# Attention scores of a one-layer language-model tower: one 32-row matmul per head instead of a zero-padded 128-row matmul per four heads

## What is computed

```python
q = _bitlinear(x, w_q).reshape(B, T, N_HEADS, D_HEAD)      # 32 sequences, T = 128, 16 heads of 32
k = _bitlinear(x, w_k).reshape(B, T, N_HEADS, D_HEAD)
v = _bitlinear(x, w_v).reshape(B, T, N_HEADS, D_HEAD)
attn = jnp.einsum('bqhd,bkhd->bhqk', q, k) * D_HEAD ** (-0.5)
attn = jax.nn.softmax(attn, axis=-1)
out = jnp.einsum('bhqk,bkhd->bqhd', attn, v).reshape(B, T, C)
return _bitlinear(out, w_o)
```

## Time and profile before

| | |
|---|---|
| median of three runs | 1735.05 us |
| span of the profiled execution (first to last instruction) | 1725.5 us |
| the rest of the time, median less span | 9.6 us |
| TensorE busy | 1609.2 us, 93% of the span |
| VectorE busy | 1195.8 us, 69% |
| ScalarE busy | 957.5 us, 55% |
| GpSimd busy | 632.1 us, 37% |
| in the attention stage, 290 to 760 us: TensorE / VectorE / ScalarE / GpSimd | 456.0 / 419.1 / 350.4 / 220.0 of 470 us |
| the copies into `KTx`, 320 to 740 us (29 sequences): GpSimd / ScalarE | 112.1 / 18.1 us |
| the score matmuls in the same stretch | 104.3 us |

### The profile page before, as it was taken

The page is one execution under the profiler, slowest core; times in us unless marked ns, Lnnn a source line. Parts: engine busy times, 40 slices in busy tenths (PEclk is TensorE's granted clock), DMA queues, the critical chain, the costliest instruction groups (busy, mean ns, idle before and its releaser), DMA issues.

```text
span 1725.5 us, 33624 instructions
## 1 busy us (share of the span) xinstructions
PE 1609.2 (93%) x10884; PEld 1354.1 (78%) x10884; DVE 1195.8 (69%) x2292; ACT 957.5 (55%) x1936; POOL 632.1 (37%) x614
## 2 busy tenths in 40 slices
PE   1798886999999999969999999999999999999997
PEld 0444444777777777749999999999999999999996
DVE  2687886999999999866343566666666666655665
ACT  4976774777777777753222355555555555522221
POOL 4655533544444444421750122222222222023343
PEclk9999999999999999989999999999999999999999
DMA  9999981000000000013111366677766777534365
GB/s 311 315 340 341 337 276 53 26 38 37 36 36 36 36 36 31 37 68 115 37 38 49 121 218 232 234 243 251 251 232 234 238 247 247 207 127 139 109 206 196
DMA packets 89868, 274.42 MB, mean 159 GB/s; under 512 B 12640, under 2 KB 13152, under 8 KB 89696
## 3 DMA queue, kind: packets, MB, share of 16 engines
q1 hardware_dynamic: 70688, 223.71, 37.5%
q0 software_dynamic: 17024, 45.97, 8.8%
q10 hardware_dynamic: 2112, 4.19, 0.8%
HBM read 228.14 MB, written 45.69 MB: 159 GB/s over the span
## 4 chain that ended last, share of the span: by engine, by line
PE 54%; DMA 1%; DVE 0%; POOL 0%; ACT 0%; issue 0%; POOLq 0%; DVEq 0%
PE up_ps L1372 12%; PE up_ps L1370 12%; PE up_ps L1371 12%; PE down_ps L1370 6%; PE down_ps L1371 6%; PE down_ps L1372 6%; PE xT_ps L1414 2%; DMA comb<-slot_rows,slot_i 0%; DVE H L1320 0%; DMA xr<-x_turned 0%; DVE xT_lo L1237 0%; POOL comb L1172 0%; ACT xT_hi L1187 0%; DVE H L1312 0%; PE route_ps L1366 0%
## 5 line engine op out<-in xcount | busy, mean ns | idle before, releaser
L1370 PE MATMUL up_ps<-xT_hi,w_hi 128*128 128x256 f32 (+1 forms) x1704 | 483.9, 284 | 8.4 <-DVE xT_lo L1237 8.4
L1372 PE MATMUL up_ps<-xT_hi,w_lo 128*128 128x256 f32 (+1 forms) x1704 | 481.1, 282 | 0.0
L1371 PE MATMUL up_ps<-xT_lo,w_hi 128*128 128x256 f32 (+1 forms) x1704 | 479.1, 281 | 0.0
L1370 PEld LDWEIGHTS up_ps<-xT_hi,w_hi 128*128 128x128 f32 (+1 forms) x1704 | 308.1, 181 | 10.0 <-DVE xT_lo L1237 8.5
L1371 PEld LDWEIGHTS up_ps<-xT_lo,w_hi 128*128 128x128 f32 (+1 forms) x1704 | 308.1, 181 | 1.2
L1372 PEld LDWEIGHTS up_ps<-xT_hi,w_lo 128*128 128x128 f32 (+1 forms) x1704 | 308.1, 181 | 0.0
L1242 DVE TENSOR_TENSOR w_lo<-w_stage,w_hi 128x1408 fp32r<-128x1408 f32 (+1 forms) x123 | 201.4, 1664 | 124.4 <-ACT w_hi L1192 124.2
L1164 POOL DMA_INDIRECT xr<-x_rows,slot_tokens x78 | 120.5, 1544 | 441.6 <-PE xT_ps L1414 362.2
L1219 ACT ACTIVATE h_hi<-h 128x256 fp32r<-128x256 f32 (+1 forms) x213 | 89.0, 418 | 239.3 <-DVE h L1335 239.3
L279 DVE TENSOR_TENSOR W<-W,norm_ps 128x1000 f32<-128x1000 f32 x128 | 147.1, 1190 | 53.5 <-PE norm_ps L354 53.3
L1215 ACT ACTIVATE act_g<-up_ps 128x256 f32<-128x256 f32 (+1 forms) x213 | 79.6, 374 | 182.8 <-PE up_ps L1372 181.4
(11 more groups left out here) (192 smaller groups left out, 2978.0 us busy)
## 6 DMA issues: line engine op xcount, KB each, us to landing
W<-table_t SPq DMA_DIRECT2D x32, 2000.0 KB, 17.2
w_stage<-packed SPq DMA_DIRECT2D x80, 704.0 KB, 6.5
w_stage<-packed SPq DMA_DIRECT2D x40, 768.0 KB, 5.2
slot_rows<-y_rows SPq DMA_DIRECT2D x39, 512.0 KB, 6.7
xr<-x_turned SPq DMA_DIRECT2D x32, 512.0 KB, 3.7
x_rows<-x SPq DMA_DIRECT2D x32, 256.0 KB, 2.0
x_turned<-x2T SPq DMA_DIRECT2D x32, 256.0 KB, 2.0
out<-H SPq DMA_DIRECT2D x32, 256.0 KB, 3.7
```

The lines of the kernel that those rows point to most:

```text
L1370: pe.matmul(out, a_hi, b_hi, start=first, stop=False)
L1371: pe.matmul(out, a_hi, b_lo, start=False, stop=False)
L1372: return pe.matmul(out, a_lo, b_hi, start=False, stop=last)
```

## The change

Q and K columns are laid out anew (on the host, by a transposition of the two weight matrices' columns): head 4j + m now lies on partitions 32j to 32j + 31 of block m, so that the four heads of one block lie on four row strips of TensorE and belong to four different groups, hence four PSUM banks. Each head's scores are a matmul of its own with 32 rows, 128 weight columns and 128 moving columns, 16 in place of 4, in the order block m outside, strip j inside. `scores_done` is raised only in the last block, once per group. `KTx`, its zeroing, its copies on GpSimd and ScalarE and their semaphores are gone; `K_T` becomes a pair of buffers.

```diff
-        K_T = sb("K_T", [P, KT, T])
-        KTx = pair("KTx", [P, KT, GROUPS, T])
+        K_T = pair("K_T", [P, KT, T])
 ...
-                if proj.yes:
-                    pool.wait_ge(K_scaled, proj.next)
-                    ...
-                    after(pool, scores_done, (proj.i - 1) * GROUPS)
-                    for n, j in enumerate(POOL_SLOTS):
-                        at = slice(DH * j, DH * (j + 1))
-                        pool.tensor_tensor(KTx[proj.b][at, :, j, :], K_T[at, :, :], ones[at, :].unsqueeze(1).to_broadcast([DH, KT, T]),
-                                           ALU.mult).then_inc(KTx_by_pool, 1)
-                        pool.wait_ge(KTx_by_pool, proj.i * len(POOL_SLOTS) + n + 1)
 ...
-                    for j in ACT_SLOTS:
-                        at = slice(DH * j, DH * (j + 1))
-                        act.activation(KTx[proj.b][at, :, j, :], K_T[at, :, :], ACT.Copy).then_inc(KTx_by_act, 1)
 ...
-                    after(dve, KTx_by_act, proj.i * len(ACT_SLOTS))
-                    after(dve, KTx_by_pool, proj.i * len(POOL_SLOTS))
                     dve.wait_ge(k_done, proj.next)
-                    dve.tensor_tensor(K_T[:, :, :], ...
+                    dve.tensor_tensor(K_T[proj.b][:, :, :], ...
 ...
                     pe.wait_ge(QT_done, score.next)
-                    pe.wait_ge(KTx_by_act, score.next * len(ACT_SLOTS))
-                    pe.wait_ge(KTx_by_pool, score.next * len(POOL_SLOTS))
+                    pe.wait_ge(K_scaled, score.next)
                     after(pe, attn_done, score.i)
-                    for j in range(GROUPS):
-                        pe.matmul(S[:, j, :], QT[score.b][:, j, :], KTx[score.b][:, j, :, :].rearrange("p j t -> p (j t)"),
-                                  start=True, stop=True).then_inc(scores_done, 1)
+                    for m in range(KT):
+                        for j in range(GROUPS):
+                            at = slice(DH * j, DH * (j + 1))
+                            mm = pe.matmul(S[:, j, m * T:(m + 1) * T], QT[score.b][at, m, :], K_T[score.b][at, m, :], start=True, stop=True)
+                            if m == KT - 1:
+                                mm.then_inc(scores_done, 1)
```

More of the change, by code:

```diff
@@ L481, in attend @@
         w_in, const_made, dve_const = sem("wr_in"), sem("const_made"), sem("dve_const")
-        KTx_zeroed = sem("KTx_zeroed")
         names = ("rows_scaled stats_done moments_done eps_added rstd_done y_done absmax_done dequant_done quant_done v_scaled z_done xq_done"
-                 " diag_done xq_turned xqT_done spread_done scale_bc_done q_done QT_done k_done K_scaled KTx_by_act KTx_by_pool v_done V_done"
+                 " diag_done xq_turned xqT_done spread_done scale_bc_done q_done QT_done k_done K_scaled v_done V_done"
                  " scores_done max_done exp_done prob_turned probT_done heads_done"
@@ L492, in attend @@
         (rows_scaled, stats_done, moments_done, eps_added, rstd_done, y_done, absmax_done, dequant_done, quant_done, v_scaled, z_done, xq_done,
-         diag_done, xq_turned, xqT_done, spread_done, scale_bc_done, q_done, QT_done, k_done, K_scaled, KTx_by_act, KTx_by_pool, v_done, V_done,
+         diag_done, xq_turned, xqT_done, spread_done, scale_bc_done, q_done, QT_done, k_done, K_scaled, v_done, V_done,
          scores_done, max_done, exp_done, prob_turned, probT_done, heads_done,
@@ L509, in attend @@
         PROBS_BANK = (1, 0, 1, 2)
-        ACT_SLOTS, POOL_SLOTS = (2,), (0, 1, 3)
         def steps(eng, body):
@@ L597, in _ @@
         def _(act):
-            def zero_KTx(b):
-                act.activation(KTx[b][:, :, :, :].rearrange("p m j t -> p (m j t)"), carried_b[:, :].to_broadcast([P, KT * GROUPS * T]),
-                               ACT.Copy).then_inc(KTx_zeroed, 1)
             def body(norm, fit, proj, score, out, route):
@@ L674, in body @@
                     act.activation(scale_bc[:, :], bank[3][:, 0:T], ACT.Copy).then_inc(scale_bc_done, 1)
-                    if isinstance(fit.i, int) and fit.i == 0:
-                        zero_KTx(1)
-            act.wait_ge(dve_const, 2)
-            zero_KTx(0)
             steps(act, body)
@@ L731, in body @@
                 if proj.yes:
-                    after(dve, KTx_by_act, proj.i * len(ACT_SLOTS))
-                    after(dve, KTx_by_pool, proj.i * len(POOL_SLOTS))
                     dve.wait_ge(k_done, proj.next)
-                    dve.tensor_tensor(K_T[:, :, :], bank[2][:, :].rearrange("p (k t) -> p k t", k=KT), bc, ALU.mult).then_inc(K_scaled, 1)
+                    dve.tensor_tensor(K_T[proj.b][:, :, :], bank[2][:, :].rearrange("p (k t) -> p k t", k=KT), bc, ALU.mult).then_inc(K_scaled, 1)
                 if score.yes:
@@ L1453, in turned, with by_row_tile @@
         return np.ascontiguousarray(np.asarray(w).T)
+    def by_row_tile(w_t):
+        return np.ascontiguousarray(w_t.reshape(D, GROUPS, PER_GROUP, DH).transpose(0, 2, 1, 3).reshape(D, D))
     gates = np.concatenate([L0_ffn_Wg, np.asarray(L0_ffn_Wsg).reshape(2, ROUTED_F, D)])
@@ L1476 @@
         "magnitude_t": turned(np.asarray(L0_tok_magnitude).reshape(KT, P)),
-        "w_q_t": turned(L0_attn_w_q), "w_k_t": turned(L0_attn_w_k), "w_v_t": turned(L0_attn_w_v), "w_o_t": turned(L0_attn_w_o),
+        "w_q_t": by_row_tile(turned(L0_attn_w_q)), "w_k_t": by_row_tile(turned(L0_attn_w_k)), "w_v_t": turned(L0_attn_w_v), "w_o_t": turned(L0_attn_w_o),
         "router_t": turned(L0_ffn_Wr),
```

2 lines of the change are left out of this document (removed).

## The result

| | before | after |
|---|---|---|
| median of four runs each | 1734.88 us (1732.93 to 1736.13) | 1895.38 us (1891.14 to 1908.99) |
| ratio, 95% interval | | 1.0947 [1.0907, 1.0988] |
| span of the profiled execution | 1725.5 us | 1895.8 us |
| attention, start of the first Q to start of the last x2 | 285.9 to 765.4 | 287.4 to 935.3 |
| experts, start of the first up to start of the last down | 778.1 to 1715.6 | 948.1 to 1885.9 |

The account below looks back on a forecast made before the run. Two rings of waits between TensorE, VectorE and ScalarE were taken to bound attention's 14.58 us step; 0.6 (strips) + 1.45 (clock) - 0.05 (copies) = 2.0 us a step, over 30 steps +60 us on 1735: 1795 us, range 1731 to 1870.

Parts of the forecast that it names:

- The two rings: Attention: two closed chains of waits among VectorE, ScalarE and TensorE; one is as long as the 14.58 us step.
- ring B: Attention: TensorE's 10.8 us from `aq` transposes to next scores, then row maxima and L743 release the next transposes; slack 0.2.
- Part 2, the strips: Attention scores: group 0 is ready later with 32-row matmuls; 0 to 1.25 us a step, 0.6 taken.
- upper bound from serial weight loads: Attention scores: if strips do not overlap, group 0 comes 0.95 us late plus 0.3 for switching; 1.25 us a step.
- Part 3, the clock: Attention: TensorE's clock falls about once a step behind the scores; 1.45 us a step taken, bounds 0 to +282 us.
- one stretch of low clock: Attention: a fall costs 1.3 to 1.5 us a step if one low stretch follows, from Q and K's 1.53.
- R4: Rival: in attention the low clock stays for whole steps; 2017 us by the upper bound; chance 0.08.
- every second step: Attention: milder case of R4, the low clock lasting through every second step; 1880 us.
- Part 1, the copies: Attention: dropping GpSimd's and ScalarE's key copies and the zeroing gains little; -1 to -5 us.
- R3: Rival: faster, as R2, and freed GpSimd also shortens VectorE's operations beside the copies in attention; 1726 us; chance 0.08.
- R1: Rival: in attention the clock holds and strips run one after another, only late group 0 costs; 1768 us; chance 0.14.
- R2: Rival: in attention the strips overlap and the clock holds, no difference to be told; 1733 us; chance 0.20.

Follow-up runs that it names:

- late signal, filled: Kernel before, all four score groups signalled with the last score matmul, plus eight full-height matmuls behind the scores: 1786.40 us, ratio 1.0289.
- filled kernel: Changed kernel plus ten full-height bf16 matmuls of 512 columns behind the scores, product never read: 1721.01 us, ratio 0.9907.
- filling among the heads: Changed kernel plus four full-height matmuls behind the first group of heads and four behind the third, none behind the scores: 1820.40 us, ratio 1.0482.
- Strip by strip: Changed kernel with score loops swapped, strip j outside and block m inside, so neighbouring heads use the same strip: 1830.95 us, ratio 1.0365.
- 32-row filling: Changed kernel plus ten matmuls of 32 rows instead of 128 behind the scores: 1759.39 us, ratio 1.0125.
- late signal: Kernel before, with all four score groups signalled together at the last score matmul: 1876.82 us, ratio 1.0781.
- moved kernel without filling: Changed kernel with GpSimd's scaling of H moved behind K's scaling, no filling matmuls: 1966.39 us, ratio 1.0874 on a chip where before took 1808.83.

## Why the prediction was wrong

**The two rings.** Right. The late signal, filled, made the step 1.64 us longer where the rings gave 1.6, and the waits of the changed kernel are those of ring B.

**Part 2, the strips.** Wrong, at little price: I took 0.6 us a step. All four strips run side by side. Read one by one in the trace, the starts of the first four L821 are 608.429, .436, .443 and .449, then the next four begin at 608.643 and the later fours every 0.112 us. In the filled kernel the scores end at 466.29 and VectorE takes its maxima from 466.83 on without a wait, so that the cost is 0. The Trainium skill, page "TensorE: Matmul & The Clock Gate", section "Part 3: Packing small matmuls — row/col tiling", has four row strips at once and, for one group of four matmuls with 512 columns, 3.07 times as fast. Here, where eight fours of 128 columns replace eight instructions of 512, it is 3.60 / 1.17 = 3.08, and the trace agrees. The upper bound from serial weight loads did not hold: the loads (181 to 187 ns each in this step) start 6.5 ns apart on the four strips, so they overlap as well.

**Part 3, the clock: the step that failed.** The prediction priced "one stretch of low clock" at 1.53 us, the time that Q and K lose. The clock did fall once in a step, 2.2 us behind the start of the `aq` transposes, and rose with K's matmuls, but the price took only what lies in the last section before the rise. Q and K did lose 1.34 us; the heads in front of them lost 4.29, and the `aq` to projection section 1.04: 6.67 us in a low stretch of 13.7, where 1.45 had been put. Between the fall and K nothing won the clock back. A fall of the price that I had put does exist, the short kind (1.56 us, under the filling among the heads); in the changed kernel the long kind came. I had written just that as R4's ground, "the heads' matmuls of 33 columns between loads may not raise it", and given it 0.08. The argument set against it, that the 32 matmuls of Q and K raised the clock at the start of the stage, is true and does not help: they do raise it, at the end of the step, and the next scores lose it again. R4's mechanism, with a low clock for two thirds of every step, was the case that came; its "every second step" gave 1880 (1735 + 141 = 1876, put roundly), and that 1895.38 lies near it is luck, since no step was low throughout. The earlier trace rows show falls with Q and K, or nothing, behind them; no row of before has the heads behind a fall, so the duration of the low stretch was an unknown with ends at 1.5 and 9.4 us a step, and I took its lower end as if it were measured.

**Part 1, the copies.** Right at equal clock: 3.2 us between the profiled executions, in the range of 1 to 5. The 10.7 us of the medians hold a part of the clock that no part of the prediction had. That freed GpSimd shortens VectorE's operations, R3's ground, came true (0.5 us a step on two of them), but ring B takes most of it up.

**The rivals.** R1 said the clock would hold where the strips are serial, since TensorE is never idle then. Strip by strip is the nearest test, and its clock fell without idle time. R1's sum has a slip: 0.95 to 1.25 less 0.1 is 1.0 in the middle, not 1.1, which gives 1765 and not 1768. R2's mechanism is the filled kernel, which came out at 0.9907 and not at 1.00. At equal clock, profile against profile, the change is worth 6.0 us, between R2's 2 and R3's 9; the rest of the 16 us by the medians goes with the clock of before, which is 0.986 to 0.987 in its other runs. So "it never falls" held for the steady steps of the one execution that was profiled, and the filling mends falls that the kernel before has in its other runs.

**The base.** The rest of the time was 2.0 us outside the span (1897.77 less 1895.8), not 9.6. The profiled execution of before was some 7 us shorter than the others of that kernel. It changed nothing in the forecast, since the same figure stood on both sides.

**What stays open.** What loses the clock is told by its ingredients (idle time of 1.7 us, quarter-height work, both), not by a rule that predicts it: the 32-row filling, strip by strip and the late signal lose it in some steps and not in others. Nor is it shown what decides between a short fall and a long one, and so why the changed kernel had the long one in every steady step.

## What to carry to other kernels

An edit that shortens work on TensorE also shortens what holds its clock: look at what follows the new gap, and if that is narrow work between weight loads, take as the upper end the price of the whole section up to the next dense one at 1.2 GHz, not the gap. Here a fall cost 1.6 us when it was short and 6.7 when it was long. Before such an edit is given up, fill the gap with full-height matmuls whose product nobody reads; here 2.3 us of them in each step turned +160 us into -16 (-6 at equal clock). And where an engine frees another, check the operations that ran beside it, for here one took little more than half as long. And compare mean clocks before a few us are put down to an edit.

## What the runs showed of the hardware that was not expected

- Matmuls of 32 rows on four strips start 6.5 ns apart, and fours follow each other in 0.112 us; 32 of them take 1.17 us in place of 3.60 for eight full ones. Only the first four keep the next waiting longer, 0.214 us, so the switch from 128 rows to 32 cost about 0.1 us.
- The clock can fall behind 1.7 us of idle time in a step although everything else is full height (late signal, in most steps), and without idle time behind the scores when these use 32 rows (strip by strip). In the changed kernel it fell in every steady step. Once down it stayed at 1.2 GHz through 13.7 us of each step, with TensorE's records busy for 13.38 of 13.60 us, mostly on narrow work.
- The same 1.7 us of idle time is followed by low stretches of 3.4 us in one kernel (filling among the heads) and of 13.7 in another (the changed one); in the late signal lengths from 3.4 to 17.1 us mix.
- The loss locks in: the changed kernel, strip by strip and the moved kernel without filling all show steps of 20.5 us one after another, over 20 in a row.
- VectorE's 128x512 float32 scaling takes 587 ns where the GpSimd operation has been moved away and 1080 beside it; the rounding to bf16 takes 416 ns and 624.
